# A vision tower with experts: Wd's two parts made in the state space's second batch, and the first item's gate made at the end of the state space

## What is computed

```python
h = _L0_tok_ref(x, ...)                                  # involution
h = concatenate([cls_tok, h], axis=1)                    # 4097 rows of 64
h = h + _L0_attn_ref(_layernorm(h), ...)                 # two scans over the rows, gelu
...
def _L0_ffn_ref(x, W1, b1, Wg, bg, Wd, bd):              # h + this, of layernorm(h)
    H = gelu(xf @ W1 + b1)
    probs = softmax(H @ Wg + bg)
    assign = argmax(probs)
    for e in range(8):
        y = H @ Wd[e] + bd[e]
        out = out + where(assign == e, probs[:, e:e + 1] * y, 0)
```

## Time and profile before

| what | value |
|---|---|
| median of 3 runs | 642.08 us (641.46 to 643.88) |
| profiled execution, its own time | 641.58 us |
| span of that execution | 640.0 us |
| mean granted clock of TensorE | 0.964 of full speed |
| busy share of the span: PE, DVE, POOL, ACT | 89%, 79%, 66%, 45% |
| experts' matmuls with Wd's parts (L1578) | 774 of 2964 matmuls, 285.6 us busy |

### The profile page before, as it was taken

The page is one execution under the profiler, slowest core; times in us unless marked ns, Lnnn a source line. Parts: engine busy times, 40 slices in busy tenths (PEclk is TensorE's granted clock), DMA queues, the critical chain, the costliest instruction groups (busy, mean ns, idle before and its releaser), DMA issues. The chain is left out here.

```text
span 640.0 us, 9633 instructions
## 1 busy us (share of the span) xinstructions
PE 568.6 (89%) x2964; PEld 429.5 (67%) x2964; DVE 504.3 (79%) x919; ACT 291.0 (45%) x822; POOL 421.3 (66%) x641
## 2 busy tenths in 40 slices
PE   0699999996464799999998999999999999999994
PEld 0377777775462688788886567777777777777672
DVE  6688888884674577888888488888888889888884
ACT  3122332215443122225666476666666776755410
POOL 1688999914544033336757168888888888898777
PEclk9999999999776899999999799999999999999998
DMA  6200000000000000000000000000000000000001
GB/s 259 59 3 0 1 2 1 0 0 2 1 0 2 0 1 1 0 1 1 2 0 1 1 1 17 18 17 17 17 18 18 16 18 3 14 18 17 18 17 33
DMA packets 13144, 9.83 MB, mean 15 GB/s; under 512 B 4524, under 2 KB 12844, under 8 KB 12844
## 3 DMA queue, kind: packets, MB, share of 16 engines
q1 hardware_dynamic: 13084, 9.29, 4.5%
q10 hardware_dynamic: 16, 0.00, 0.0%
HBM read 5.10 MB, written 4.20 MB: 15 GB/s over the span
## 5 line engine op out<-in xcount | busy, mean ns | idle before, releaser
L1578 PE MATMUL ex_pE<-ex_WdP,ex_hid 128*128 128x512 f32 (+1 forms) x516 | 183.9, 407 | 0.0
L1578 PEld LDWEIGHTS ex_pE<-ex_WdP,ex_hid 128*128 128x128 f32 (+1 forms) x516 | 96.5, 187 | 32.4 <-issue 10.8
L1821 POOL TENSOR_TENSOR ex_s<-ex_ms 128x1024 f32<-128x1024 f32 (+1 forms) x33 | 83.4, 2529 | 47.6 <-DVE ex_ms L1699 47.4
L1699 DVE TENSOR_TENSOR ex_ms<-ex_pE,ex_gate 128x512 f32<-128x512 f32 x129 | 87.7, 681 | 30.1 <-PE ex_pE L1578 30.0
L816 DVE TENSOR_TENSOR inv_prod<-inv_pW,m_img 128x504 f32<-128x504 f32 x144 | 91.7, 681 | 17.3 <-PE inv_pW L731 15.6
L1578 PE MATMUL ex_pE<-WdL,ex_hid 128*128 128x512 f32 x258 | 101.7, 394 | 0.0
L742 PE MATMUL inv_pS<-ident,inv_prod 128*128 128x128 f32 x576 | 87.7, 275 | 4.8 <-DVE inv_prod L816 4.8
L742 PEld LDWEIGHTS inv_pS<-ident,inv_prod 128*128 128x128 f32 x576 | 69.9, 141 | 27.3 <-DVE inv_prod L816 19.3
L1445 POOL TENSOR_TENSOR hT<-hT,m_M 128x512 f32<-128x512 f32 x24 | 34.0, 1427 | 67.5 <-ACT m_M L1395 67.5
L731 PE MATMUL inv_pW<-inv_ysb,m_conv2L 98*128 98x512 f32 x144 | 69.3, 484 | 2.3 <-DVE inv_ysb L804 2.3
L279 DVE TENSOR_TENSOR ex_hid<-ex_hidf,ex_hid 128x512 fp32r<-128x512 f32 (+1 forms) x64 | 61.0, 972 | 0.0
(11 more groups left out here) (248 smaller groups left out, 1126.0 us busy)
## 6 DMA issues: line engine op xcount, KB each, us to landing
m_img<-in_x SPq DMA_DIRECT2D x2, 2048.0 KB, 9.3
out<-ex_res SPq DMA_DIRECT2D x16, 256.0 KB, 2.3
WdT<-in_L_ffn_Wd SPq DMA_DIRECT2D x2, 256.0 KB
bd<-in_L_ffn_bd SPq DMA_DIRECT2D x16, 2.0 KB
W1d<-in_L_ffn_W SPq DMA_DIRECT2D x2, 64.0 KB
m_Bm<-in_L_attn_fwd_B_real SPq DMA_DIRECT2D x2, 16.0 KB, 2.0
m_Bm<-in_L_attn_fwd_B_imag SPq DMA_DIRECT2D x2, 16.0 KB, 2.1
m_Bm<-in_L_attn_bwd_B_real SPq DMA_DIRECT2D x2, 16.0 KB, 2.1
```

The source lines that it names most:

```text
L1578: last = nc.tensor.matmul(pE[n % 3][0:P].rearrange("p e f -> p (e f)"), hid[i % 2][value][:, h, par, 128 * j:128 * j + P], WdP[weight][:, ...
L1699: nc.vector.tensor_tensor(ms[b % NB][0:P, t % TPB, :].rearrange("p (e f) -> p e f", e=EX), pE[n % 3][0:P], gate[i % 2][0:P, t, :].unsqueez ...
L1821: nc.gpsimd.tensor_tensor(s4[0:P, 0:T], m[:, :, 0:4 * F], m[:, :, 4 * F:], ALU.add).then_inc(halved, 1)
```

## The change

Two things are changed. GpSimd makes `Wd`'s parts in the second batch: the cast stands behind the additions of step 4, the subtraction behind those of step 5. And item 0 is judged in the state space: `judge` stands behind the last `leave`, `gates` behind the last `leave_class`, ScalarE's `add_bg` behind its last gelu of rows, VectorE's `choose_best` and `weigh_best` and ScalarE's tanh at the end of their lists. The banks of the state space (`pV`) and its tensor `back[0]` take the logits of item 0. To have room for that, the gate's tensors move into the place of the last batch's normed rows (`piece`, value 0, batch 3), and the second buffer of the hidden layer, which lay there, gets a place of its own. The waits of item 1 on what item 0 had used fall away, since item 0 uses other buffers.

```diff
+        self.gl = late("gl", [128, 5, T, EX])
+        self.hot = [late(f"hot{n}", [128, 2, T, EX]) for n in range(2)]
+        self.gate = [late(f"gate{n}", [128, T, EX]) for n in range(2)]
...
+    def judge(self, pe, i, bank, hid):
+        pe.wait_ge(self.parted, 4 * i + 4)
...
+    def add_bg(self, act, i, level, bank):
+        act.wait_ge(self.judged, i + 1)
...
+    def gates(self, pe, i, bank, level):
+        pe.wait_ge(self.leveled, i + 1)
...
                     leave(b, s)
+                    if not more:
+                        pe.wait_ge(f.gelued, 4)
+                        f.judge(pe, 0, pV[0][1], f.hid0)
                     leave_class(b)
+                    if not more:
+                        f.gates(pe, 0, pV[1][0], back[0])
...
                 f.low(v, 1, pV[0][0])
+                f.choose_best(v, 0, pV[1][0])
+                nc.vector.memset(f.inverse[:, :, EX:], -float(EX)).then_inc(f.consts, 1)
+                v.wait_ge(f.consts, 1)
+                f.weigh_best(v, 0)
...
+                            if not more:
+                                f.add_bg(act, 0, back[0], pV[0][1])
...
+                f.tanh(act, 0)
...
-                    if k == 4:
+                    if k == -3:
                         nc.gpsimd.tensor_copy(f.WdP[0][:], ...).then_inc(f.wg_high, 1)
...
-                    if k == 6:
-                        pool.wait_ge(f.wg_high, 2)
+                    if k == -2:
+                        pool.wait_ge(f.wg_high, 1)
                         nc.gpsimd.tensor_tensor(f.WdP[1][:], ..., f.WdP[0][:], ALU.subtract).then_inc(f.wd_parted, 1)
...
-        hid = [f.hid0, [g.piece(f"ex_hid1{t}", t, 3, 0, [128, 2, 2, CH], F32R) for t in range(2)]]
+        hid = [f.hid0, [sb(f"hid1{t}", [128, 2, 2, CH], F32R) for t in range(2)]]
...
-                    if i == 0:
-                        gates(0)
...
-                judge(0)
...
-                add_bg(0)
...
-                    if i == 0:
-                        tanh(0)
...
-                choose_best(0)
-                weigh_best(0)
```

More of the change, by code:

```diff
@@ L152, in __init__, with late @@
         self.bdP = g.bdP
+        at = [0]
+        def late(name, shape):
+            at[0] += math.prod(shape[1:])
+            return g.piece("ex_" + name, 0, 3, at[0] - math.prod(shape[1:]), shape, F32)
+        self.gl = late("gl", [128, 5, T, EX])
+        self.hot = [late(f"hot{n}", [128, 2, T, EX]) for n in range(2)]
+        self.gate = [late(f"gate{n}", [128, T, EX]) for n in range(2)]
+        self.inverse = late("inverse", [128, T, EX + 1])
+        self.gs = late("gs", [128, 4, T])
+        self.best = [late(f"best{n}", [128, T]) for n in range(2)]
         self.hflat = g.hT[:].rearrange("p b r q -> p (b r q)")
@@ L279, in part @@
         self.nc.vector.tensor_tensor(low, whole, high, ALU.subtract).then_inc(self.parted, 1)
+    GATE = 11
+    def judge(self, pe, i, bank, hid):
+        pe.wait_ge(self.parted, 4 * i + 4)
+        if i == 0:
+            pe.wait_ge(self.wg_parted, 1)
+        n = 0
+        for value in range(2):
+            for h in range(2):
+                for par in range(2):
+                    last = self.nc.tensor.matmul(bank[0:4 * EX, 0:self.cols(i)], self.WgP[:, value, par, h, :],
+                                                 hid[value][:, h, par, 0:self.cols(i)], start=(n == 0), stop=(n == 7))
+                    n += 1
+        last.then_inc(self.judged, 1)
@@ new lines, in add_bg @@
+    def add_bg(self, act, i, level, bank):
+        act.wait_ge(self.judged, i + 1)
+        self.nc.scalar.activation(level[0:4 * EX, 0:self.cols(i)], bank[0:4 * EX, 0:self.cols(i)], ACT.Identity,
+                                  bias=self.g.bgc[:, 0:1]).then_inc(self.leveled, 1)
+    def gates(self, pe, i, bank, level):
+        pe.wait_ge(self.leveled, i + 1)
+        for j in range(self.columns(i)):
+            last = self.nc.tensor.transpose(bank[0:self.rows(i), 32 * j:32 * j + 32],
+                                            level[0:4 * EX, 128 * j:128 * j + self.rows(i)], self.g.ident[0:4 * EX, 0:4 * EX])
+        last.then_inc(self.gated, 1)
@@ new lines, in tanh, with choose_best @@
+    def tanh(self, act, i):
+        act.wait_ge(self.dv, self.GATE * i + 3)
+        P, T = self.rows(i), self.groups(i)
+        self.nc.scalar.activation(self.gl[0:P, 2, 0:T], self.gl[0:P, 0, 0:T], ACT.Tanh, scale=0.5).then_inc(self.tanhed, 1)
+    def choose_best(self, v, i, pL):
+        P, T = self.rows(i), self.groups(i)
+        G = lambda n: self.gl[0:P, n, 0:T, :]
+        s = lambda n: self.gs[0:P, n, 0:T]
+        wide = lambda a: a.unsqueeze(2).broadcast_to([P, T, EX])
+        base = self.GATE * i
+        v.wait_ge(self.gated, i + 1)
+        logits = pL[0:P, 0:32 * self.columns(i)].rearrange("p (t v e) -> p t e v", v=2, e=EX)
+        self.nc.vector.tensor_reduce(G(3), logits, AX.X, ALU.add).then_inc(self.dv, 1)
+        v.wait_ge(self.dv, base + 1)
+        self.nc.vector.tensor_reduce(s(0), G(3), AX.X, ALU.max).then_inc(self.dv, 1)
+        v.wait_ge(self.dv, base + 2)
+        self.nc.vector.tensor_tensor(G(0), G(3), wide(s(0)), ALU.subtract).then_inc(self.dv, 1)
+        v.wait_ge(self.dv, base + 3)
+        self.nc.vector.scalar_tensor_tensor(out=G(1), in0=G(0), scalar=0.0, in1=self.g.rank[0:P, :].unsqueeze(1).broadcast_to([P, T, EX]),
+                                       op0=ALU.is_ge, op1=ALU.mult).then_inc(self.dv, 1)
+        v.wait_ge(self.dv, base + 4)
+        self.nc.vector.tensor_reduce(s(1), G(1), AX.X, ALU.max).then_inc(self.dv, 1)
+        v.wait_ge(self.dv, base + 5)
+        if i >= 2:
+            v.wait_ge(self.gate_turned, i - 1)
+        both = lambda a: a.unsqueeze(1).broadcast_to([P, 2, T, EX])
+        self.nc.vector.tensor_tensor(self.hot[i % 2][0:P, :, 0:T, :], both(G(1)),
+                                s(1).unsqueeze(1).unsqueeze(3).broadcast_to([P, 2, T, EX]), ALU.is_equal).then_inc(self.dv, 1)
@@ new lines, in weigh_best @@
+    def weigh_best(self, v, i):
+        P, T = self.rows(i), self.groups(i)
+        G = lambda n: self.gl[0:P, n, 0:T, :]
+        s = lambda n: self.gs[0:P, n, 0:T]
+        base = self.GATE * i
+        v.wait_ge(self.tanhed, i + 1)
+        v.wait_ge(self.dv, base + 6)
+        self.nc.vector.tensor_scalar(G(4), G(2), -0.5, 0.5, ALU.mult, ALU.add).then_inc(self.dv, 1)
+        v.wait_ge(self.dv, base + 7)
+        self.nc.vector.reciprocal(self.inverse[0:P, 0:T, 0:EX], G(4)).then_inc(self.dv, 1)
+        v.wait_ge(self.dv, base + 8)
+        self.nc.vector.tensor_reduce(s(2), self.inverse[0:P, 0:T, :], AX.X, ALU.add).then_inc(self.dv, 1)
+        v.wait_ge(self.dv, base + 9)
+        self.nc.vector.reciprocal(self.best[i % 2][0:P, 0:T], s(2)).then_inc(self.dv, 1)
+        v.wait_ge(self.dv, base + 10)
+        self.nc.vector.tensor_tensor(self.gate[i % 2][0:P, 0:T, :], self.hot[i % 2][0:P, 0, 0:T, :],
+                                self.best[i % 2][0:P, 0:T].unsqueeze(2).broadcast_to([P, T, EX]), ALU.mult).then_inc(self.dv, 1)
@@ L1458, in experts @@
     NB = TPI // TPB
-    GATE = 11
+    GATE = f.GATE
     with ExitStack() as ctx:
@@ L1649, in add_bg @@
                 def add_bg(i):
[L1650 to L1651 removed]
+                    if i >= 2:
                         act.wait_ge(gated, i)
[L1653 to L1659 removed]
+                    f.add_bg(act, i, level, pGR)
                 def rest(i):
```

95 lines of the change are left out of this document (13 added, 82 removed).

## The result

The changed kernel takes 646.09 us in the median (644.77 to 647.57, 8 runs), the kernel before 643.56 (641.46 to 643.98, 8 runs on the same chip); the ratio is 1.0049, with a 95% interval of 1.0035 to 1.0063. By the ratio that is 3.1 us slower (the two medians lie 2.5 us apart), where +1.1 and "within 0.5%" were forecast. The time lies in the range that I gave and the ratio just inside the 0.5%, but its whole interval lies above 1: the change is a real loss, nearly three times the forecast one, and the forecast of no measurable difference was wrong.

The account below looks back on a forecast made before the run. TensorE, busy 89% of the span, was taken as the bound. Terms -2.0 - 1.8 + 1.9, the gate (0.0 in all up to the hiding), +1.5 - 0.4 made +1.1: 642.7, given as 643.2 us in the median; range 640.2 to 646.4.

Parts of the forecast that it names:

- Parts 1 and 2: Step 15: without the subtraction the last states come sooner, -2.0 us; the fifteen matmuls behind run at high clock, -1.8.
- Rival C: Step 15: another wait replaces the 2.52 us stop, parts 1 and 2 bring nothing, 647.0 us; chance 0.08.
- part 6: Experts' first window: transposes leave it and item 1's judge no longer waits, -0.4 us; GpSimd's later additions cost nothing.
- Part 3: Second batch: Wd's cast and subtraction hold up VectorE, so step 7's states come late and TensorE loses +1.9 us.
- Rival A: Second batch hides Wd's parts, part 3 is nothing: 641.3 us, or 640.5 with the clock back sooner; chance 0.24.
- Rival B's first form: Step 7: TensorE's stop brings the clock down, 645.0 us, or 646.6 with GpSimd's full time; rival B's chance 0.18.
- Part 4: Last leave to hiding of item 1: the uncovered gate chain and meeting take 7.9 us; with parts 1 to 3, 0.0.
- Part 5: Behind the meeting: after TensorE's standstill of about 4 us, hiding of item 1 and first tiles run cold, +1.5 us.
- Rival B's second form: Behind the meeting: the low clock lasts for a second stretch, the same sum as the first form; rival B's chance 0.18.

Follow-up runs that it names:

- wd_alone: Kernel before with only the making of Wd's parts moved to the second batch, the gate left as it was: 642.68 us, ratio 0.9989.
- wd_spread: Kernel before with Wd's cast and a halved subtraction spread over the third batch, the gate as before: 639.86 us, ratio 0.9969.
- after_fillers: Changed kernel plus twelve matmuls without use, three ahead of the transposes and nine following VectorE's gate chain: 643.62 us, ratio 1.0003.
- gate_alone: Kernel before with only item 0's gate moved to the end of the state space, Wd's parts left in the last batch: 645.54 us, ratio 1.0044.
- spread_judge: Kernel before with Wd's parts spread over the third batch and only judge and its bias of item 0 ahead of the meeting: 640.10 us, ratio 0.9947.
- spread_warm: Kernel before with Wd's parts spread over the third batch and seven matmuls without use behind the class step: 638.32 us, ratio 0.9923.
- spread_judge_warm: Wd's parts spread, only judge and bias ahead of the meeting, plus seven matmuls without use behind the class step: 639.77 us, ratio 0.9947.

## Why the prediction was wrong

**Parts 1 and 2 were right.** The last states' stop fell from 2.52 to 0.41, or -2.1 for the -2.0; the fifteen matmuls behind it ran at full clock, -1.6 for -1.8. Rival C, another wait in its place, did not come. wd_alone shows both without the gate. It also shows that part 6's "GpSimd's later additions none either" holds only behind the gate's chain: without it the meeting waits for them, 0.5 us longer.

**Part 3 was right in its mechanism, 0.3 short in size.** The subtraction met L1395 as I said, at 2.83 for the assumed 2.72, and so did the cast; the delay is 2.22 for 1.9 and stays to the end. Rival A, which hid it, failed: the subtraction began 0.12 us ahead of L1395. Rival B's first form failed too, the clock staying high at step 7 behind a stop of 1.44. That the price goes by where the two engines meet, and not by the amount of work, wd_spread shows: the same work, in halves and in the third batch, costs TensorE 0.3 us, though VectorE is held up there too. Cutting the subtraction and moving it were not tried apart. In the changed kernel L1395 ended 0.55 us after the cast (268.44 for 267.89) and 0.55 after the subtraction (278.70 for 278.15). The Trainium skill, SBUF — State Buffer, SBUF: two separate sides, which rival A cites, has it so that of the two engines the one that starts later waits for the whole of the other's instruction. The trace agrees. What decided was only where the subtraction fell.

**Part 4 is the step that failed.** It counts the class step, "behind which ScalarE's bias is done", and goes on with the transposes. ScalarE works its list in order, and in the changed code the bias is written behind ScalarE's wait for the class step's result. So the class step hid nothing: bias, transposes and the signals between them came after it. `judge` to hiding took 8.46 us for the forecast 7.9. With the bias moved it is 7.47, so the other terms of that sum were 0.4 too large, and the one omitted is worth 1.0. The order of ScalarE's instructions in the kernel's code says it: that `add_bg` stands "behind its last gelu of rows" is true, but `act.wait_ge(yielded, b * YPB + n + 1)`, here the wait for the class step, stands between the two. I read VectorE's and TensorE's lists there and not ScalarE's.

**Part 5 was mis-sized, and moving the bias mends it.** I took +1.5 for the low clock and -0.4 for part 6; measured is 6.52 less 4.22, or +2.3, since TensorE worked for over 5.4 us at the low level, where I had taken one stretch of some 3.3. Rival B's second form, in which the low level lasts a second stretch, is what happened. But with the bias moved the stretch is 5.27 to 5.42, or +1.05 to +1.2, the forecast's +1.1, behind the same standstill. That the clock costs this time is shown by after_fillers, in which the low level is over by the first tile and the hidings stand 3.93 us apart. Why 0.8 us less between the class step and the transposes shortens the low level, no run says; that stays open. The late place of the bias alone does not set its length: gate_alone, with the bias as late and the same 3.83 us of standstill, took 5.92. The forecast's remark that the price could be "near to nothing or twice as large", by the Trainium skill, TensorE: Matmul & The Clock Gate, Part 1, came near for the changed kernel (+2.7, with part 6 taken out) and for the first execution of spread_judge (7.11 for 4.21); what it implied, that it would vary from execution to execution, four traces of the changed kernel did not show and two of spread_judge did.

**The sum.** Net, at the second hiding, 0.4 us from parts 1 to 3, 0.6 from part 4 and 1.2 from parts 5 and 6 come on top of the forecast's +1.1, all on one side, and make +3.2. The kernel with the bias moved has the forecast's sum, ratio 1.0019 or +1.2; in part that is luck, as 0.4 too little from parts 1 to 3 and 0.4 too much in part 4 cancel. I had given a loss of over 0.5% a chance of 0.14. Rival B names a second low stretch, but no rival of mine was the order of ScalarE's list.

## What to carry to other kernels

Before an operation counts as hidden, find it in its own engine's list and read what wait stands ahead of it: an operand that is ready helps nothing behind a wait for something else. A serial chain of small instructions belongs behind a meeting of blocks, where other work covers it, and not ahead of it, where everyone waits; and a long GpSimd instruction beside a VectorE that is nearly due should be put, perhaps in pieces, where the step has slack. Where TensorE stands still at a meeting, a few matmuls without use can be worth as much as the work moved there, as long as they put the meeting off by less than the clock gives back: by 0.4 us in spread_warm, which gained 1.2, but by 1.3 us in spread_judge_warm, where the ratio did not change.

## What the runs showed of the hardware

The low level of TensorE's clock does not go by the length of the standstill alone. Behind 3.83 us the next two hidings stood 6.5 us apart in four executions of one program, 5.3 to 5.4 in three of another that differs in one instruction's place, and 5.9 in the one execution of gate_alone; behind 0.96 us, 7.1 and 5.8. The level can also fall after the standstill is over: in one execution 1.6 us into TensorE's work, which it then slowed for 3.4 us. And the meeting of the engines itself takes time: from the end of the last engine's work to the first matmul of the next block it was 0.45 to 0.5 us, whether GpSimd was last (359.50 to 360.00 in wd_alone), VectorE (365.17 to 365.64 in the changed kernel) or TensorE itself (0.45 in spread_warm).
